# Graph network kernel: edge features and edge times multiplied per edge ahead of the scatter, with the copies of that work placed inside the ranking step

## What is computed

```
# before this, three times: g + deg_pos * (neigh_mean @ Wl + h @ Ws) + b, elu; then x = layernorm(x + h)
ei = concat([edges, edges reversed, self loops])   # ef, stf, et come twice, then the loops' rows
node_i, node_j = ei[:, 0], ei[:, 1]
seg_sum  = segment_sum([node_feature[node_i], stf], node_i)
source_node_vec = seg_sum / max(cnt, 1)
target_vec = concat([node_feature[node_j], ef, et])        # 64 + 64 + 64
neighbor_emb = target_vec @ W1.T + b1
neighbors_sum = relu(segment_sum(neighbor_emb, node_i))
out = concat([neighbors_sum, source_node_vec]) @ W2.T + b2
x = layernorm(x + out)
```

## Time and profile before

| | us |
|---|---|
| median of 3 runs (11109.44 to 11128.29) | 11116.84 |
| the profiled execution | 11130.16 |
| its span on the profile | 11128.4 |

### The profile page before, as it was taken

One profiled execution on the slowest core, in us unless ns is written; L12 is line 12 of the kernel. 1 busy time (PEld: TensorE's weight loads), 2 busy tenths in 40 slices (PEclk: granted clock), 3 DMA queues, 4 the chain that ended last, 5 costly groups with the idle time before them and its releaser, 6 DMA issues.

```text
span 11128.4 us, 191621 instructions
## 1 busy us (share of the span) xinstructions
PE 6864.9 (62%) x46640; PEld 6050.2 (54%) x46640; DVE 6383.6 (57%) x15194; ACT 3581.3 (32%) x10119; POOL 5207.2 (47%) x4833
## 2 busy tenths in 40 slices
PE   7899977800039999556465664556635566656665
PEld 6688867800028888444345554455534455445555
DVE  8899972300036666444575555755567555665556
ACT  0233320000027777333392113921129411481111
POOL 0068887866644444666005661056610366206650
PEclk9999999999999999777697776977769887897776
DMA  9965555555569989556396663966629766896670
GB/s 384 388 179 144 144 144 124 123 142 139 139 176 304 302 297 294 164 166 162 91 396 216 192 188 100 393 220 191 188 51 354 270 191 192 262 361 194 192 172 12
DMA packets 1567388, 2320.61 MB, mean 209 GB/s; under 512 B 974516, under 2 KB 1046056, under 8 KB 1567320
## 3 DMA queue, kind: packets, MB, share of 16 engines
q1 hardware_dynamic: 1227608, 1356.73, 36.5%
q0 software_dynamic: 292608, 911.36, 29.7%
q10 hardware_dynamic: 47104, 51.75, 1.9%
HBM read 1328.55 MB, written 986.78 MB: 208 GB/s over the span
## 4 chain that ended last, share of the span: by engine, by line
issue 28%; PE 22%; DVE 19%; another core or an unknown queue 9%; DMA 9%; ACT 7%; DVEq 5%; ACTq 1%; POOL 1%; SPq 0%; POOLq 0%
PE ps L759 8%; DMA gathered<-ring 5%; PE ps L736 4%; DVE mask L1309 3%; PE ps L836 3%; ACT ring L1074 2%; DVEq L371 2%; ACT hring L1084 2%; PE ps L752 2%; DVE node L1500 2%; DMA frows<-by_src 2%; DVE ohj L1227 1%; DVE oh_s L1368 1%; DVE prod L1293 1%
## 5 line engine op out<-in xcount | busy, mean ns | idle before, releaser
L650 POOL DMA_INDIRECT ring<-gathered,gidx x2176 | 2170.3, 997 | 3328.7 <-DMA gathered<-ring 2118.5
L580 POOL DMA_INDIRECT by_src<-prow,ppos x1562 | 1958.2, 1254 | 1228.5 <-DMA ppos<-pos 707.2
L1382 DVE TENSOR_REDUCE red<-ps 128x256 f32<-128x768 f32 x680 | 650.0, 956 | 1645.5 <-remote 1227.7
L1462 DVE CAST ring<-ps 128x384 bf16<-128x384 f32 x2176 | 1087.5, 552 | 367.7 <-PE ps L752 346.6
L752 PE MATMUL ps<-hring,oht_g 128*128 128x192 bf16 x8704 | 872.4, 246 | 614.9 <-DVE ring L1462 204.7
L836 PE MATMUL ps<-ring,oht_g 128*128 128x192 bf16 x8704 | 1075.5, 286 | 174.7 <-issue 117.5
L759 PE MATMUL ps<-frows,oh_s 128*128 128x193 f32 x2176 | 658.4, 470 | 837.2 <-issue 565.5
L1074 ACT CAST ring<-ps 128x384 bf16<-128x384 f32 x2176 | 1124.5, 519 | 10.6 <-PE ps L752 10.4
L836 PEld LDWEIGHTS ps<-ring,oht_g 128*128 128x128 bf16 x8704 | 954.7, 127 | 291.3 <-issue 251.6
L752 PEld LDWEIGHTS ps<-hring,oht_g 128*128 128x128 fp8e4 x8704 | 659.0, 97 | 828.3 <-issue 786.1
L719 PE MATMUL ps<-snap,oht_e 98*128 98x98 f32 x3130 | 1056.4, 441 | 0.0
(11 more groups left out here) (226 smaller groups left out, 12892.2 us busy)
## 6 DMA issues: line engine op xcount, KB each, us to landing
gathered<-ring SPq DMA_DIRECT2D x544, 768.0 KB
by_src<-zeros SPq DMA_DIRECT2D x34, 6272.0 KB, 46.3
frows<-by_src SPq DMA_DIRECT2D x544, 392.0 KB
oht_g<-oht SPq DMA_DIRECT2D x544, 256.0 KB, 6.2
gathered<-got SPq DMA_DIRECT2D x136, 776.0 KB
prow<-in_edge_attr_n SPq DMA_DIRECT2D x284, 352.0 KB
bc<-tidrow ACTq DMA_DIRECT2D x313, 160.0 KB
prow<-in_edge_attr SPq DMA_DIRECT2D x142, 352.0 KB
```

Source lines behind the costliest of these rows:

```text
L580: pool.indirect_dma_start(out=table, out_offset=bass.IndirectOffsetOnAxis(ap=ppos[:, s, j:j + 1], axis=0), in_=prow[:, s, j, :], in_offset ...
L650: pool.indirect_dma_start(out=ring[:, c, :], out_offset=None, in_=gb, in_offset=offsets(g, c % 4)).then_inc(q.got[g], 16)
L1382: return dve.tensor_reduce(red[:, u, :, 0:D], four_of(bank)[:, :, 0:HW].rearrange("p e (a d) -> p e d a", d=D), AX.X, ALU.add)
L1462: dve.tensor_copy(ring[:, c, 2 * HW:4 * HW], ps[:, 2 * (c % 4) + 1, 0:2 * HW]).then_inc(q.gv, 1)
```

## The change

Per edge, z = [ef, et] @ W1's two parts for them (128 x 64) is made before the scatter, so that a row of `by_src` is z, `stf` and four words: ROW 196 to 132 words (528 B), FEAT 193 to 129. For that:
- The buffers have 6 columns (PB), and a *unit* of work is 3 columns (UC); there are 521 units. SP loads `ef` and `et` into `praw` (three buffers) and `stf`, `meta` and `ppos` into `prow`. PE turns three columns (`raw_turned`, f32 transposes), ACT copies them to `rawT` (`raw_kept`), PE multiplies (`z_product`, three f32 matmuls of 64 columns), ACT copies into `prow` (`z_kept`), and POOL's scatter waits for that (`s_z`).
- 312 units stand in the ranking, one per step; 204 in the moves, six per turn of four groups; five behind.
- ACT's `z_kept` waits until the buffer's earlier scatters have landed (`s_pout`), in the middle of a ranking step.
- `last` adds z, already multiplied, through an identity block in `w_n2`, and gives `unit` the weights that `et` had.

```diff
+ZF, STF, ONE, LS, LD, ROW = 0, D, 2 * D, 2 * D + 1, 2 * D + 2, 2 * D + 4
+PB = 6
+UC = 3
@@ sync
+            def raw(s, use, cols, first=False):
+                if not first:
+                    sp.wait_ge(s_rawt, 6 * use + (2 * s - 4))
+                for f, c in ((ef, 0), (et, D)):
+                    sp.dma_start(praw[:, s, 0:cols, c:c + D], v[...]).then_inc(s_raw[s], 16)
+            sp.wait_ge(s_tids, 2)
+            for s in range(3):
+                raw(s, 0, PB, True)
+            sp.wait_ge(s_pos, 4)
...
+            with sp.Fori(1, RANKED) as i:
+                for s in range(3):
+                    if s == 0:
+                        sp.wait_ge(s_pos, 4 * i + 4)
+                    row(s, i, PB)
+                    raw(s, i + 1, PB)
@@ gpsimd
             def scatter(s, use):
-                pool.wait_ge(s_plod[s], use * 80 + 80)
+                pool.wait_ge(s_plod[s], use * 48 + 48)
+                pool.wait_ge(s_z, 6 * use + (2 * s + 2))
@@ tensor
+            def raw_turned(n, v, bank, s, use, first=False):
+                pe.wait_ge(s_raw[s], 32 * use + 32)
+                if not first:
+                    pe.wait_ge(s_rawc, n - 1)
+                for j in range(UC):
+                    mm = pe.transpose(ps[:, bank + u, j * P:(j + 1) * P], praw[:, s, UC * h + j, :], ident[:, :])
+            def z_product(n, v, bank, first=False):
+                pe.wait_ge(s_rawc, n + 1)
+                if not first:
+                    pe.wait_ge(s_z, n - 1)
+                for j in range(UC):
+                    mm = pe.matmul(ps[:, bank + 2 + u, j * D:(j + 1) * D], rawT[:, u, j * P:(j + 1) * P], w_z[:, :], ...)
@@ rank, tensor
+                    if l == 1 and not (begin and u == 0):
+                        z_product(n - 1, u + 5, 4, begin and u < 3)
+                    if l == 3 and m is not None:
+                        raw_turned(n, u, 4, u // 2, m, begin and u < 2)
@@ moves, tensor
+                    for v in range(6):
+                        if v in (0, 2, 3, 5):
+                            moves(4 * m + (0, 0, 1, 2, 0, 3)[v], (0, 0, 1, 0, 0, 1)[v])
+                        raw_turned(n, v, 0, v // 2, m + use)
+                        if not first or v > 0:
+                            z_product(n - 1, v + 5, 0)
@@ scalar
+            def z_kept(n, v, bank, s, use, first=False):
+                act.wait_ge(s_zmm, n + 1)
+                if not first and h == 0:
+                    act.wait_ge(s_pout[s], use * (PB * 16))
@@ rank, scalar
                     act.copy(snap[0:T, (u * LANES + l) % 2, :], ps[0:T, 0, 0:T]).then_inc(s_snap, 1)
+                    if l == 4 and m is not None:
+                        raw_kept(n, u, 4, turn == 0 and u < 2)
+                    if l == 2 and u > 0:
+                        z_kept(n - 1, u - 1, 4, (u - 1) // 2, m, turn == 0)
@@ last, vector
-                    dve.tensor_scalar(cat[:, :, D:P], facc[:, ts, EF:EF + D], 1.0, None, ALU.mult)
+                    dve.tensor_copy(cat[:, :, D:P], unit_t)
-                    dve.tensor_tensor(cat2[:, :, 0:D], facc[:, ts, ET:ET + D], unit_t, ALU.add)
+                    dve.tensor_scalar(cat2[:, :, 0:D], facc[:, ts, ZF:ZF + D], 1.0, None, ALU.mult)
```

More of the change, by code:

```diff
@@ L251, in build @@
         s_pout = [sem(f"s_pout{u}") for u in range(3)]
[L252 to L253 removed]
+        s_raw = [sem(f"s_raw{u}") for u in range(3)]
+        s_rawt = sem("s_rawt")
+        s_rawc = sem("s_rawc")
+        s_zmm = sem("s_zmm")
+        s_z = sem("s_z")
         s_wload = sem("s_wload")
@@ L586, in _ @@
                 scatter(s, 0)
-            with pool.Fori(1, TAIL_PB) as i:
+            with pool.Fori(1, PTURNS) as i:
                 for s in range(3):
                     scatter(s, i)
-            scatter(0, TAIL_PB)
-            pool.wait_ge(s_prest, 80)
+            for s in range(2):
+                scatter(s, PTURNS)
+            pool.wait_ge(s_plod[2], PTURNS * 48 + 96)
+            pool.wait_ge(s_z, UNITS)
             pool.nop(nofuse=True)
-            pool.indirect_dma_start(
-                out=table, out_offset=bass.IndirectOffsetOnAxis(ap=ppos[0:REST, 1, 0:1], axis=0),
-                in_=prow[0:REST, 1, 0, :], in_offset=None).then_inc(s_prout, 16)
+            for j in range(UC):
+                to_table(2, j, P if j < UC - 1 else REST)
             def offsets(g, c):
@@ L976, in rank, with beside_moves @@
                     tile_ids(n + 3, u % 3)
-            for u in range(6):
-                rank(u, u, u == 0)
-            with act.Fori(1, STEPS // 6 - 1) as m:
+            for turn in range(2):
                 for u in range(6):
-                    rank(6 * m + u, u, False)
-            for n in range(STEPS - 7, STEPS):
-                rank(n, n % 6, False, n + 3 >= STEPS)
+                    rank(6 * turn + u, u, turn, turn)
+            with act.Fori(2, STEPS // 6 - 1) as m:
+                for u in range(6):
+                    rank(6 * m + u, u, m)
+            for n in range(STEPS - 7, STEPS - 1):
+                rank(n, n % 6, n // 6, last=n + 3 >= STEPS)
+            rank(STEPS - 1, 0, None, last=True)
+            def beside_moves(m, first=False):
+                for v in range(6):
+                    raw_kept(6 * m + v, v, 0)
+                    if v > 0:
+                        z_kept(6 * m + (v - 1), v - 1, 0, (v - 1) // 2, m)
+                    elif not first:
+                        z_kept(6 * m - 1, 5, 0, 2, m - 1)
+            beside_moves(UNITS_R // 6, True)
+            with act.Fori(UNITS_R // 6 + 1, PTURNS) as m:
+                beside_moves(m)
+            for v in range(5):
+                raw_kept(6 * PTURNS + v, v, 0)
+                if v > 0:
+                    z_kept(6 * PTURNS + v - 1, v - 1, 0, (v - 1) // 2, PTURNS)
+                else:
+                    z_kept(6 * PTURNS - 1, 5, 0, 2, PTURNS - 1)
+            z_kept(UNITS - 1, 4, 0, 2, PTURNS)
             def indices(q, j, g):
```

152 lines of the change are left out of this document (89 added, 63 removed).

## The result

The changed kernel takes 11301.57 us (median of 4 runs, 11287.96 to 11305.22), the kernel before 11114.13 us (median of 4): a ratio of 1.016, 95% interval 1.015 to 1.018. It is 187 us slower where 114 us faster was forecast. The time lies in the forecast's range, on the other side of no change.

| stretch | before, us | changed, us | difference | forecast |
|---|---|---|---|---|
| start to first scatter | 634.1 | 442.6 | -191 | -180 |
| end of ranking (last count copy) | 1598.5 | 2415.7 | +817 | +855 |
| last `cmp` of the moves | 2182.7 | 3384.2 | +1202 | |
| last scatter | 3188.5 | 3429.7 | +241 | +210 |
| first gather by destination | 3238.6 | 3477.1 | +238.5 | +210 |

A forecast was written before the change was run, and what follows sets the result against it. POOL's 1562 scatters were taken to set the end up to 3190 us. 11130 + 210 (front) - 228 (by destination) - 109 (sums) = 11003, 10990 after a 13 us median correction, stated as 11,000 us; range 10,590 to 11,380.

The forecast's parts named there:

- Start: Before the ranking: shorter clears, ranking starts 60 us later at 420 us, scatters some 180 us sooner, first near 450.
- Clock: Ranking and moves: PE stays at 1.2 GHz, f32 passes of 421 ns, all added PE work at that price.
- clock up: Rival, ranking: denser PE work brings 2.4 GHz, step 5.2 us, 407 us less, 10,590 us; chance 0.17.
- Ranking's step: Ranking: a chain of PE and ACT makes a step 6.5 us, 313 steps 2035 us, end at 2455 us.
- Moves: Moves after the ranking: 27 us per turn of four groups, bounds 26 and 30; 34 turns 918 us.
- the rival in part: Rival, moves: POOL issuing back to back stalls other engines, 11.4 us per turn, 388 us, total 11,390; chance 0.23.
- The front part as a whole: Start to last scatter: 210 us slower, last scatter at 3398 us against 3188.
- By destination: Stage by destination: PE's block falls 0.39 us, ACT needs 1.65; block 2.22 to 1.8 us, -228 us, bounds 1.65 and 2.0.
- The sums: Four sums: shorter `feature_sum` and fetch save 0.2 us per turn, bounds 0 and 0.6; -109 us in all.
- the third rival: Rival, ranking: new work is hidden and scatters end at 2978 us; excluded as no case of its own, no chance given.
- The sign: Whole kernel: +210 in front, -228 and -109 behind, so faster; chances faster 0.57, same 0.05, slower 0.38.

The follow-up runs named there:

- one_product: The changed kernel with one f32 product per unit in place of three, ACT's copy the same size: 11028.6 us, ratio 0.995 to the kernel before.
- some_pauses: The kernel before with 0.65 us POOL pauses, behind every second gather by destination, one in four by source and in the sums: 11052.89 us, ratio 0.996.
- short_ohf: The changed kernel with ACT's copy of the one hots by destination cut to a quarter, PE's passes unchanged: 11207.41 us, ratio 1.011 to the kernel before.
- narrow_rows: The changed kernel without z (ef in its place; transposes, products, copies left out), rows still 132 words: 10933.86 us, ratio 0.981 to the kernel before.
- some_pauses_after: The changed kernel with scatters in threes, each waiting for its own unit, plus the pauses of some_pauses: 11128.88 us, ratio 1.003 to the kernel before.
- threes_paused: The changed kernel with scatters in threes, each waiting for its own unit, and a 0.65 us POOL pause behind each three: 11297.67 us, ratio 1.015.

## Why the prediction was wrong, point by point

- **Start: right.** First scatter at 442.6 (forecast near 450), ranking from 417.
- **Clock: right.** 421 ns passes and 0.50 throughout; added transposes and products did not lift it. The rival "clock up" didn't happen. The Trainium skill (TensorE: Matmul & The Clock Gate, "Part 4: PE-mode transpose") would give the same, but two thirds of the added passes are products (3126 of 4689), so this doesn't test its rule. Its 275 ns is the duration of one transpose; here one lasts 0.42 us, but the next starts 0.21 us after it (three in 0.84 us), and the step pays the 0.21.
- **Ranking's step: right in size** (6.39 us, forecast 6.45 and 6.5), 39 us early at the stage's end. Its bound was told too much by ACT: one_product gave 0.69 of 0.86 us and PE is busy for 1814 of 1997 us, so it is mostly PE's own work with short waits between.
- **Moves: the rival in part.** 28.6 us per turn against 27, inside my 26 to 30, some 50 us in all (the last columns behind them took 20 us more as well). The chain puts 5.0 us per turn on the standstills, 17.6% of 944 us in 33 turns, which I had put at either nothing or 11.4 us. My argument against them, that they don't occur in the moves before, rested on one trace. In some_pauses, whose code is the same up to there, DVE waited 595.7 us for nothing named between 1604 and 2603, 44.5 us at longest.
- **The front part as a whole** came out some 30 us beside my 210, and part of that is luck: the ranking ended 39 us early, and moves and last columns took back some 70.
- **By destination: the step that failed.** I took 0.39 us out of PE's block of 1.91, said that ACT's 1.65 is late next and rounded up to 1.8. It measured 2.12, where my worst bound was 2.0. The mistake was to lay a mean (2.22) beside the work of one engine: the mean held standstills, DVE's register load and waits for landing that no engine's busy time shows, and these don't shrink with PE. short_ohf, narrow_rows and some_pauses_after show it: 0.11 us for ACT's 0.36, 0.07 for the short row alone, 0.15 for the pauses. PE's own gain was also smaller than my 0.39: a block's weight loads take 0.97 us where I had 0.89. 180 us of the miss lie here. Even with pauses and the short row a block takes 1.97 us by the starts of its gathers; what holds the rest was not taken apart further.
- **The sums: the second.** 4 us each instead of 27. I had written that POOL needs 5.2 of 6.3 us and that PE is idle 39%, and still took 0.2 us for PE without a row that puts `feature_sum` on the chain. My lower bound, nothing, was nearly the answer. What does set a turn stays open: one pause more of POOL per turn costs nothing (some_pauses), and 47% of the chain is "issue" and unnamed. 93 us.
- **A slip without effect:** the 2978 us in the third rival should be 2991, 3398 less 407.
- **The sign** hung on these two terms: +239 in front against -64 behind, where I had +210 against -337.

What stays open: what it is that the other engines lack in a standstill, and whether POOL's issuing takes it or the transfers that it starts, since a pause thins out both. The length of a row doesn't decide it alone: in the moves of the kernel before POOL issued 262 scatters without a pause, and unnamed waits came to 5.5 us. The profile gives the waits no name.

## What to carry to other kernels

A stage whose mean per block is well above every engine's work is held by something that has no busy time; find it (here in the chain of waits, as "unknown" and "issue") before crediting a smaller row or a shorter matmul with its share. Where POOL issues indirect DMAs back to back, look at the neighbours' unnamed waits: if POOL has time to spare, pauses that it really waits for, here at every second gather by destination and at one in four behind, made the kernel before 0.4% faster; where they make POOL the bound, they cost most of their length (0.54 of 0.65 us in the sums). And new work that is put under a loop that PE already fills is not hidden there: it cost 388 us here, though the tail of lone scatters, 1000 us with PE idle before, was gone in return.

## What the runs showed of the hardware that was not expected

- 24 indirect DMAs of POOL without a pause, the last 15 of them 1.27 us apart (one_product): PE down to one pass per 1.4 to 2.1 us, DVE without a start for 17 us with its input ready, ACT for 3.2, and all three resume within 0.6 us of each other, some 3.2 us after POOL's last. After three gathers in a row by destination ACT's wait was 2.1 us, about once in eight blocks (59 times, 124 us).
- 0.95 us between the end of one issue and the next, behind every three scatters or every second gather by destination, takes these waits to zero (threes_paused, some_pauses); the usual 0.30 us, with or without a memset of 0.17 in it, doesn't (7.6 and 8.1% of the chain).
- The same program shows quite different standstills from run to run where they are under cover: the moves of the kernel before ended at 2183 us, and at 2336 and 2603 in two kernels whose code up to there is the same, with the last scatter at 3188, 3181 and 3181.
